# Row shift on GpSimd, one power for two deviations, and transposes, logits and routing one turn later

## The reference

```python
x = x + tanh(g_xattn[0]) * L0_xattn(layernorm(x), ctx, ctx, mask)   # one head, layernorm on the context, gain and beta
x = x + tanh(g_ffn[0])   * L0_ffn(layernorm(x))                      # shared network + one of 8 experts a row (argmax of logits)
x = x + tanh(g_xattn[1]) * L1_xattn(layernorm(x), ctx, ctx, pad)     # 16 heads, relative bias
x = x + tanh(g_ffn[1])   * L1_ffn(layernorm(x))                      # one of 8 matrices a row
```

```python
context = softmax(scores) @ V
x = x + tanh(g) * ((context - mu) * rsqrt(var + EPS) * ln_gamma + ln_beta)
logits = layernorm(x) @ router.T ; expert = argmax(logits)
```

## Time and profile before

| | us |
|---|---|
| median of 3 runs | 523.37 |
| lowest and highest run | 522.79, 527.62 |
| the profiled execution | 525.38 |
| its span, first to last instruction | 523.6 |
| TensorE busy in the span | 482.2 |
| VectorE busy | 386.9 |
| GpSimd busy | 346.6 |
| ScalarE busy | 300.5 |

### The profile page before, as it was taken

One profiled execution on the slowest core, in us unless ns is written; L12 is line 12 of the kernel. 1 busy time (PEld: TensorE's weight loads), 2 busy tenths in 40 slices (PEclk: granted clock), 3 DMA queues, 4 the chain that ended last, 5 costly groups with the idle time before them and its releaser, 6 DMA issues.

```text
span 523.6 us, 12435 instructions
## 1 busy us (share of the span) xinstructions
PE 482.2 (92%) x3408; PEld 303.7 (58%) x3408; DVE 386.9 (74%) x1178; ACT 300.5 (57%) x981; POOL 346.6 (66%) x813
## 2 busy tenths in 40 slices
PE   6977888799999999879999999999999999999993
PEld 5967776455655666655555555555555555555441
DVE  2879998667333334345899999999999999999852
ACT  3746665322254555266776776676766767776630
POOL 5554777777244555462778787888878787878532
PEclk9979897899999999987999999999999999999997
DMA  8885350022144322100000000000000000000000
GB/s 233 161 113 157 92 160 12 16 77 62 45 106 120 82 74 68 47 11 7 11 13 22 21 12 21 13 21 11 22 13 21 16 19 21 13 17 10 7 6 16
DMA packets 33924, 25.77 MB, mean 49 GB/s; under 512 B 8105, under 2 KB 31281, under 8 KB 33825
## 3 DMA queue, kind: packets, MB, share of 16 engines
q1 hardware_dynamic: 30864, 19.48, 15.3%
q0 software_dynamic: 2272, 4.67, 2.8%
q10 hardware_dynamic: 720, 0.83, 0.6%
HBM read 16.89 MB, written 8.39 MB: 48 GB/s over the span
## 4 chain that ended last, share of the span: by engine, by line
PE 48%; DVE 2%; issue 1%; POOL 1%; POOLq 0%; ACT 0%; DVEq 0%
PE bank L1376 13%; PE bank L1325 8%; PE bank L1311 8%; PE bank L1301 6%; PE bank L1392 2%; PE bank L1362 2%; PE bank L1297 2%; PE bank L1358 1%; PE bank L1342 1%; PE bank L1346 1%; PE bank L1337 1%; PE bank L1287 1%; PE bank L1381 1%; PE bank L1283 1%; PE bank L1398 1%
## 5 line engine op out<-in xcount | busy, mean ns | idle before, releaser
L1439 ACT ACTIVATE wgu<-wgu,top 128x77 f32<-128x77 f32 x256 | 67.4, 347 | 15.7 <-DVE top L1541 15.7
L1376 PE MATMUL bank<-w,xn3T 128*128 128x512 f32 x128 | 71.7, 644 | 0.1
L1449 ACT ACTIVATE PRT<-bank 128x512 f32<-128x512 f32 (+1 forms) x128 | 54.5, 426 | 29.0 <-PE bank L1311 28.5
L983 POOL DMA_INDIRECT routed<-ys,to x39 | 37.4, 960 | 43.7 <-DVE ys L1186 35.0
L1311 PE MATMUL bank<-cst,wgu 128*128 128x128 f32 x320 | 60.2, 286 | 1.6 <-ACT wgu L1439 1.3
L1531 DVE TENSOR_TENSOR wgu<-bank,biasQ 128x616 f32<-128x616 f32 x64 | 50.9, 795 | 7.0 <-PE bank L1301 5.6
L1325 PE MATMUL bank<-PRT,VP 128*32 128x128 f32 x1024 | 55.0, 287 | 0.7 <-ACT PRT L1449 0.7
L1541 DVE TENSOR_REDUCE top<-wgu 128x8 f32<-128x616 f32 x64 | 50.2, 784 | 1.1
L1301 PE MATMUL bank<-KB,QT 32*128 32x308 f32 x256 | 50.2, 433 | 0.0
L1181 DVE TENSOR_TENSOR hid<-actg,bank 128x256 f32<-128x256 f32 x39 | 16.4, 421 | 41.8 <-ACT actg L1090 41.8
L1311 PEld LDWEIGHTS bank<-cst,wgu 128*128 128x128 f32 x320 | 37.7, 142 | 16.1 <-issue 13.2
(11 more groups left out here) (232 smaller groups left out, 1261.6 us busy)
## 6 DMA issues: line engine op xcount, KB each, us to landing
xs<-sorted_x SPq DMA_DIRECT2D x39, 64.5 KB, 1.8
wgu<-in_wgu SPq DMA_DIRECT2D x4, 512.0 KB
y<-routed SPq DMA_DIRECT2D x32, 64.0 KB, 1.8
out<-res SPq DMA_DIRECT2D x32, 64.0 KB, 1.7
ctxT<-in_ctxT SPq DMA_DIRECT2D x16, 77.0 KB, 3.0
mask<-in_mask SPq DMA_DIRECT2D x16, 77.0 KB, 3.8
wdn<-in_wdn SPq DMA_DIRECT2D x2, 512.0 KB
X<-in_x SPq DMA_DIRECT2D x1, 768.0 KB, 5.5
```

The costliest lines, as they stand in the source:

```text
L983: nc.gpsimd.indirect_dma_start(routed, bass.IndirectOffsetOnAxis(ap=to[:, t:t + 1], axis=0), ys[t % WAYS][:, :], None).then_inc(st_y[t % W ...
L1376: nc.tensor.matmul(map_bank(b, k)[:, :], xn3T[u][:, :], w2[:, k * HT:(k + 1) * HT, :], start=True, stop=True).then_inc(s["f"], 1)
L1439: last = nc.scalar.activation(SC[u][:, head, :], SC[u][:, head, :], ACT.Exp, bias=top[u][:, head:head + 1])
L1449: nc.scalar.activation(PT[half][:, k], bP[end][:, 0:k.stop - k.start], ACT.Exp if half else ACT.Copy).then_inc(s["pTs"], 1)
```

## The change

GpSimd now adds the shift (`shifted`, 128 x 256 numbers a pair) in place of VectorE. The two inverse deviations that GpSimd takes in one turn, that of the new rows of pair g and that of the context of pair g + 1, lie side by side in one tile and come from one power of 128 x 4; `inv_std0` and `inv_std1` become `context` (squares and variance of the next pair) and `inv_std`. The order within GpSimd's turn is now: context of g + 1, epsilon and mean of g, power, product of g, an inversion of a piece if one is due, the shift of g + 2, and a scatter. Before the first turn it adds two shifts and takes the context's power of pair 0. On TensorE, `norm1_T`, `logits` and their warming matmuls go from lag 7 to 8 and `ranks` from 8 to 9, on ScalarE the copy `norm1_T` from 6 to 7, on VectorE `route` and `slots` from 10 to 11.

```diff
-        written_out(NG, [(before({14: 7, 15: 3}), 7), (norm1_T, 7), (rows_T, 1), (values, 3), (weigh, 4), (before({15: 6}), 4),
-                         (keys, 0), (probs_T, 3), (ranks, 8), (scores, 1), (before({13: 2, 14: 2, 15: 2}), 7), (logits, 7), (unit, 18)])
+        written_out(NG, [(before({14: 7, 15: 3}), 8), (norm1_T, 8), (rows_T, 1), (values, 3), (weigh, 4), (before({15: 6}), 4),
+                         (keys, 0), (probs_T, 3), (ranks, 9), (scores, 1), (before({13: 2, 14: 2, 15: 2}), 8), (logits, 8), (unit, 18)])
...
-        written_out(NG, [(unit, 19), (values_1, 3), (norm1, 6), (probs_T, 3), (keys, 0), (exps, 2), (rows_T, 0), (norm1_T, 6)])
+        written_out(NG, [(unit, 19), (values_1, 3), (norm1, 6), (probs_T, 3), (keys, 0), (exps, 2), (rows_T, 0), (norm1_T, 7)])
...
-        def shifted(g):
-            dve.wait_ge(s["xT"], g + 1)
-            x = X[:, pair(g), :]
-            nc.vector.tensor_tensor(x, x, spread(shift), ALU.add).then_inc(s["sh"], 1)
...
-        written_out(NG, [(route, 10), (values_0, 5), (attend_stats, 6), (shifted, 5), (centred, 6), (residual, 7), (masked, 3), (slots, 10), (mask_bias, 0), (unit, 20)])
+        written_out(NG, [(route, 11), (values_0, 5), (attend_stats, 6), (centred, 6), (residual, 7), (masked, 3), (slots, 11), (mask_bias, 0), (unit, 20)])
...
-        def inv_std0(g):
+        def shifted(g):
+            pool.wait_ge(s["xT"], g + 1)
+            x = X[:, pair(g), :]
+            nc.gpsimd.tensor_tensor(x, x, spread(shift), ALU.add).then_inc(s["sh"], 1)
+
+        def context(g):
             u = g % 2
             pool.wait_ge(s["umv"], g + 1)
             wait(pool, s["zg"], g - 1)
-            then(nc.gpsimd.tensor_tensor(vr[u][:, :], es[u][:, :], es[u][:, :], ALU.mult))
-            then(nc.gpsimd.tensor_tensor(vr[u][:, :], vr[u][:, :], mv[u][:, :, 1], ALU.add))
-            nc.gpsimd.tensor_tensor(ru[u][:, :], vr[u][:, :], power[:, 0:PAIR], ALU.pow).then_inc(s["inv"], 1)
-            if g + 4 < NG and piece_of(g + 4) > 3 and piece_of(g + 4) != piece_of(g + 3):
-                invert(piece_of(g + 4))
-
-        def inv_std1(g):
-            u = g % 2
+            wait(pool, s["xn1"], g - 2)
+            then(nc.gpsimd.tensor_tensor(esq[u][:, :], es[u][:, :], es[u][:, :], ALU.mult))
+            nc.gpsimd.tensor_tensor(vr[u][:, 0:PAIR], esq[u][:, :], mv[u][:, :, 1], ALU.add).then_inc(s["iv"], 1)
+            step[0] += 1
+
+        def inv_std(g):
+            u, n = g % 2, (g + 1) % 2
+            if g == 0:
+                pool.wait_ge(s["w0"], 4)
+                shifted(0)
+                shifted(1)
+                context(0)
+                pool.wait_ge(s["iv"], step[0])
+                nc.gpsimd.tensor_tensor(ru[0][:, 0:PAIR], vr[0][:, 0:PAIR], power[:, 0:PAIR], ALU.pow).then_inc(s["inv"], 1)
+            if g + 1 < NG:
+                context(g + 1)
             pool.wait_ge(s["xmv"], g + 1)
             wait(pool, s["xn1"], g - 1)
-            count(nc.gpsimd.tensor_tensor(ve1[u][:, :], mv1[u][:, :, 1], eps[:, 0:1].to_broadcast([128, PAIR]), ALU.add))
+            count(nc.gpsimd.tensor_tensor(vr[n][:, PAIR:2 * PAIR], mv1[u][:, :, 1], eps[:, 0:1].to_broadcast([128, PAIR]), ALU.add))
             then(nc.gpsimd.tensor_tensor(nm1[u][:, :], mv1[u][:, :, 0], minus[:, 0:1].to_broadcast([128, PAIR]), ALU.mult))
-            then(nc.gpsimd.tensor_tensor(r1[u][:, :], ve1[u][:, :], power[:, 0:PAIR], ALU.pow))
-            nc.gpsimd.tensor_tensor(nb1[u][:, :], nm1[u][:, :], r1[u][:, :], ALU.mult).then_inc(s["inv1"], 1)
+            k = slice(0 if g + 1 < NG else PAIR, 2 * PAIR)
+            nc.gpsimd.tensor_tensor(ru[n][:, k], vr[n][:, k], power[:, k], ALU.pow).then_inc(s["inv"], 1)
+            pool.wait_ge(s["inv"], g + 2)
+            nc.gpsimd.tensor_tensor(nb1[u][:, :], nm1[u][:, :], ru[n][:, PAIR:2 * PAIR], ALU.mult).then_inc(s["inv1"], 1)
+            if g + 5 < NG and piece_of(g + 5) > 3 and piece_of(g + 5) != piece_of(g + 4):
+                invert(piece_of(g + 5))
+            if g + 2 < NG:
+                shifted(g + 2)
...
-        written_out(NG, [(inv_std0, 0), (inv_std1, 1), (moved, 4)])
+        written_out(NG, [(inv_std, 0), (moved, 3)])
```

More of the change, by code:

```diff
@@ L401, in attend_0 @@
     es = [sb(f"es{u}", [128, PAIR]) for u in two]
-    vr = [sb(f"vr{u}", [128, PAIR]) for u in two]
-    ru = [sb(f"ru{u}", [128, PAIR]) for u in two]
+    esq = [sb(f"esq{u}", [128, PAIR]) for u in two]
+    vr = [sb(f"vr{u}", [128, 2 * PAIR]) for u in two]
+    ru = [sb(f"ru{u}", [128, 2 * PAIR]) for u in two]
     z = [halves(units["sg"][u], 0) for u in two]
@@ L406, in attend_0 @@
     mv1 = [sb(f"mv1{u}", [128, PAIR, 2]) for u in two]
-    ve1 = [sb(f"ve1{u}", [128, PAIR]) for u in two]
     nm1 = [sb(f"nm1{u}", [128, PAIR]) for u in two]
-    r1 = [sb(f"r1{u}", [128, PAIR]) for u in two]
     nb1 = [sb(f"nb1{u}", [128, PAIR]) for u in two]
@@ L520, in scores @@
             wait(pe, s["sm"], g)
-            wait(pe, s["wh"], 2 * ((g - 11) // (QB // PAIR)) + 1)
+            wait(pe, s["wh"], 2 * ((g - 12) // (QB // PAIR)) + 1)
             pe.wait_ge(s["xTs"], g + 1)
@@ L546, in norm1_T @@
             wait(pe, s["xT2s"], g)
-            pe.wait_ge(s["xTs"], min(g + 6, NG))
+            pe.wait_ge(s["xTs"], min(g + 7, NG))
             for b in range(PAIR):
@@ L559, in ranks @@
             if i == QB // PAIR - 1 and q < NQ - 1:
-                wait(pe, s["sm"], min(g + 7, NG))
+                wait(pe, s["sm"], min(g + 8, NG))
                 if q == NQ - 2:
@@ L660, in norm1 @@
                 last = nc.scalar.activation(XN[:, PAIR * g + b, 0:D], X[:, PAIR * g + b, :], ACT.Identity,
-                                            bias=nb1[g % 2][:, b:b + 1], scale=r1[g % 2][:, b:b + 1])
+                                            bias=nb1[g % 2][:, b:b + 1],
+                                            scale=ru[(g + 1) % 2][:, PAIR + b:PAIR + b + 1])
             last.then_inc(s["xn1"], 1)
@@ L665, in norm1_T @@
             act.wait_ge(s["xT2"], g + 1)
-            act.wait_ge(s["xT"], min(g + 7, NG))
+            act.wait_ge(s["xT"], min(g + 8, NG))
             nc.scalar.activation(XNT[:, pair(g), :], bT2[:, 0:PAIR * S].rearrange("p (b s) -> p b s", b=PAIR),
```

## The result

The changed kernel takes 527.03 us as the median of 20 runs (525.52 to 531.27), the kernel before 523.56 on the same chip (20 runs). The ratio is 1.0072, with a 95% interval of 1.0056 to 1.0088: 3.5 us slower, where 1.4 us faster was forecast. The profiled execution took 527.66 us with a span of 525.9 (before: 525.38 and 523.6).

What follows compares the result with a forecast made beforehand. VectorE's turn of 4.29 us was taken as the bound, GpSimd close behind. Gains and losses of 0.7 - 0.9 + 1.4 - 0.3 + 0.45 = 1.35, rounded 1.4 us, gave 522.0 us from 523.37; range 518.0 to 526.3.

Steps and rivals of the forecast that it cites:

- Transposes, logits, routing one turn later: TensorE's turn no longer begins waiting on normalised rows of the same VectorE turn; 0.7 us regained.
- Both chains start 1.4 us earlier and keep their length: End of the first attention: remaining scatters and dense feed-forward both start 1.4 us earlier, lengths unchanged.
- step 3: Inversion of the last 12 batches: masked(10) waits 1.55 us for it; 0.9 us lost.
- step 5: Last three turns, to the end of residual(15)'s statistics: GpSimd sets the pace, 11.85 us against 11.56; loss 0.3.
- Step 1: Start up to VectorE's mask-load wait, ending at 36.13 us: nothing gained.
- Step 2: Turns from the mask wait to the end of residual(5)'s statistics: 3 x 0.24 = 0.7 us earlier.
- x(5): End of VectorE's statistics of residual(5), forecast at 54.2 us against 54.92 before.
- Step 4: The five turns up to the end of residual(12)'s statistics: about 1.4 us gained.
- x(12): End of VectorE's statistics of residual(12), forecast at 88.3 us against 89.53 before.
- Step 6: GpSimd's last product ends about 1.5 us behind residual(15)'s statistics instead of 1.95: 0.45 us gained.
- A slower clock at the dense start: Rival: first dense matmuls run at 1.2 GHz for 5 us, losing 2.5 us: 524.5 us, chance 0.13.
- The other three: Rivals: GpSimd's turns spend the gain, 523.9 us, 0.22; shift holds up VectorE, 530.6, 0.09; VectorE bounds throughout, 518.5, 0.11.

Runs made afterwards that it cites:

- e1: The changed kernel with all lags as before, so the GpSimd part alone; ratio to before 0.9974.
- e14: The GpSimd part with the later turn for pairs 11 to 15 alone and the old turn for pairs 0 to 10; ratio to before 1.0040.
- e12: Changed kernel, last four pairs' logits in their own bank, third group's ranks two turns later, copies of pairs 12 to 15 before the next normalization; ratio 1.0031.
- e11: The kernel before, unaltered, for a second profile; no ratio given, first dense matmul at 107.07 us.
- e3: The changed kernel with VectorE's routing of the third group alone put back by one turn; ratio to before 1.0089.
- e6: The changed kernel once more, unaltered, for a second profile; ratio to before 1.0081.
- e10: The changed kernel with the last four pairs' logits in another PSUM bank, ranks at their place; ratio to before 1.0056.

## Why the prediction was wrong

**The accounts.** Against before: the GpSimd part alone -0.26% (e1). The end adds 2.2 to 3.7 us in the profiles (9.8 to 10.2 in the two of after, against 6.5 to 7.6 in the five without the lags), and 3.5 us in the runs (1.0040 of e14 against 0.9974 of e1). The way adds 2.9 us in the profiles and 3.0 in the runs (1.0031 of e12 against 0.9974). Added to e1 that is 5.1 to 6.6 us; measured are 5.1 to 5.6 (1.0072 and 1.0081 against 0.9974). By the intervals each of the two differences from the runs has some 2 us of play, so the sum agrees but does not fix the parts.

**The step that failed** is "Transposes, logits, routing one turn later ... I count 0.7 us back", with the sentence that closes the sum: "Both chains start 1.4 us earlier and keep their length". I saw that TensorE's wait on fresh rows goes away, and priced that. I did not ask what then stands *ahead* of each pair's transposes. A stage that is one turn later lies, in its engine's order, behind the next pair's work, and at the end of the loop the next pair's work is exactly what is late: the third routing stands behind the residual of pair 14 on VectorE, the ranks wait for it on TensorE with the transposes of pairs 13 to 15 queued behind, and the copies stand behind the next normalization on ScalarE. The chain from the last residual to the dense network did not keep its length: it grew from 7.0 to 10.2 us. Nor did the waits of TensorE go away. In e1 it waits 9.3 us between 36 and 108 for normalised rows and 3.0 at the ranks, in after nothing for the rows and 7.8 at the ranks. On the way the later routing uncovers the wait for the inversion; this 1.6 us was in the sum (step 3), the waits for values that TensorE has late were not. The rows for the end were at hand: the ranks already waited 2.09 us for the third routing in the profile of before (at 96.21), and the lists of turns show what stands behind them. The remark that "the slots of the third group ... are inside step 5" looked at VectorE only.

**Step by step.**
- Step 1 right: the mask wait stayed, though it ended 1.5 us earlier (34.65 against 36.13), which the walk did not foresee; e11 shows that this is the scatter of single executions.
- Step 2: a turn of 4.10 us, as forecast (4.29 - 0.24 = 4.05), and one of 4.30. x(5) came at 52.9 instead of 54.2, by luck: the mask was 1.5 earlier. From the mask on, 0.55 us are gained, not 0.7.
- Step 3 right: the stall at masked(10) was 1.59, forecast 1.55. e1, in which the routing covers it at its old place, has no such wait.
- Step 4 over-sized: from x(5) to x(12) 35.5 us instead of 34.1. Seven turns of 4.10 instead of 3.98 make 0.8 of the difference, and 0.8 are two waits of VectorE on TensorE for values and context (0.36 at 84.55, 0.44 at 85.41) that before had once, behind x(12), and after has twice. The early mask hid it: x(12) at 88.4, forecast 88.3. The three profiles with the old turn there take 32.8 to 34.5.
- Step 5 right in its sum, 11.6 us to x(15) against 11.85, but partly by luck: of the waits on the shared power forecast for the last three turns only the last is there (0.55 at 98.34), and two waits for values, 1.7 us of routing and a residual that is 0.5 longer fill the rest.
- Step 6 right: the last product ends 1.5 us behind x(15).

**The rivals.** "A slower clock at the dense start" had the sign and named TensorE, but the wrong place, and a wait for GpSimd where it was one for VectorE's routing: the dense matmuls ran at 2.4 GHz from the first (1.08 us, as in the earlier trace rows); the 1.2 GHz lay ahead of them, from 97.0 to 103.9. By the pairs at the same clock it carries 0.6 to 1.1 us of the loss at the end. The other three do not decide: the shift took 0.70 to 0.77 us and not 1.29, it held up VectorE's residual in one turn and not in each, and masked(10) did wait (1.59), so VectorE did not bound throughout. The kernels with the same way whose x(15) came at 101 to 104 lost it at waits for the mask or for values (e3 at its routing too), not in GpSimd's turns.

**What stays open.** In the runs the kernels with the later turn on the way have a mean granted clock of 0.952 to 0.961, those without it 0.965 to 0.970 (e14 0.966). TensorE's waits between 36 and 108 us add up to about 13 us in both after and e1, but the longest is 4.0 in after and 2.6 in e1. That the clock on the way is a cause of its own is not shown: in the pair e6 and e14 the 2.9 us there are accounted for by two waits, one of which may itself come from it. Why the clock at the end stays low longer in some profiles than in others is open too.

## What to carry to other kernels

Before a stage is moved one turn later, write out what it then stands behind on *each* engine of its chain, and do this for the last turns of the loop as well as for a steady one: the wait that vanishes in each steady turn can come back, larger, in the drain (the turns in which the pipeline empties). A step that waits for another engine (here the ranks, for the routing) holds all that is queued behind it; giving it another buffer changed nothing that the runs tell (e10), moving it and the copies did (e12). And an inverse view of the profile finds such a thing quickly: for each late instruction, compare the end of what it depends on with its own start.

## What the runs showed of the hardware

A GpSimd instruction held up a VectorE instruction with two SBUF inputs, in the order for which the prediction had no example. VectorE's residual of pair 14, two instructions, took 1.11 us instead of 0.61. The shift began during the first of them (0.38 us); the second took 0.81 and ended 0.15 us behind the shift:

```profile
94.14 1.11 DVE L779 SCALAR_TENSOR_TENSOR X<-sg,ru,X 128x128 f32<-128x128 f32 x2
```

```profile
94.33 0.77 POOL L886 TENSOR_TENSOR X<-X,rows 128x256 f32<-128x256 f32 x1
```

The Trainium skill's "SBUF — State Buffer", section "Who interferes with whom", has such a pair exclude each other for the whole instruction, whoever starts first. The trace agrees for the second instruction, held to the shift's end; the first and the shift overlap by 0.19 us in it, which the rule does not give. It cost 0.5 us once in after, not in each turn; the shift itself took 0.70 to 0.77 us, near the shorter of the two durations of the nearest row.
